# Where scale and shift of the second layer normalisation are applied: on rows by GpSimd, or on transposed columns by ScalarE

## The reference

```python
x = x + tanh(g_xattn) * attention(layernorm(x), ctx, ctx, ...)   # first normalisation: no scale, no shift
x = x + tanh(g_ffn) * experts(layernorm(x), ...)                 # inside experts, once more:
#   mu, var over the 256 features of a token
#   xn = (xf - mu) / sqrt(var + 1e-5) * ln_gamma + ln_beta       # second normalisation, scale and shift per feature
#   logits = xn @ Wr.T ; softmax ; top 2 of 8 experts per token
#   buf[expert, slot] = xn[token]        (640 slots for each expert)
#   h = silu(buf @ Wg) * (buf @ Wu) ; y = h @ W3.T
#   out[token] += weight * y             (two experts for each token)
```

## Time and profile before

| | us |
|---|---|
| median of 3 runs | 553.26 (552.57 to 554.41) |
| span of the profiled execution, first to last instruction | 547.9 |
| median less span: what lies around the instructions | 5.4 |

### The profile page before, as it was taken

How to read it: one execution, slowest core, us unless ns; L and a number is a source line. 1 busy time by engine, 2 the same in 40 slices (tenths; PEclk the granted TensorE clock), 3 DMA queues, 4 the chain that set the end, 5 groups by cost and what they waited for, 6 DMA issues and landing times. The chain is left out here.

```text
span 547.9 us, 10716 instructions
## 1 busy us (share of the span) xinstructions
PE 474.1 (87%) x3469; PEld 436.0 (80%) x3469; DVE 378.4 (69%) x942; ACT 299.3 (55%) x756; POOL 210.1 (38%) x271
## 2 busy tenths in 40 slices
PE   5599998899989776219979999999999999999990
PEld 4388887677767664219979999998999989999990
DVE  6878989999998998736758584484853757644340
ACT  3689778687778763316546463373732736424130
POOL 8536768687868556420120303202132021221121
PEclk9899999999999998559999999999999999999996
DMA  8858331314132511164626463255551554111011
GB/s 272 203 129 211 67 75 46 77 41 78 49 70 67 195 51 52 38 215 144 214 40 211 97 214 93 25 140 162 142 166 19 136 173 136 18 18 16 11 19 19
DMA packets 41137, 56.80 MB, mean 104 GB/s; under 512 B 3721, under 2 KB 38064, under 8 KB 39040
## 3 DMA queue, kind: packets, MB, share of 16 engines
q1 hardware_dynamic: 34656, 48.10, 30.2%
q0 software_dynamic: 6144, 8.07, 8.7%
q10 hardware_dynamic: 288, 0.00, 0.0%
HBM read 36.24 MB, written 16.19 MB: 96 GB/s over the span
## 5 line engine op out<-in xcount | busy, mean ns | idle before, releaser
L544 POOL DMA_INDIRECT out_tokens<-ysc,rows x32 | 50.6, 1581 | 252.8 <-DVE ysc L1142 181.0
L1431 PE MATMUL bank<-bXh,wh 128*128 128x384 f32 (+1 forms) x384 | 123.1, 321 | 7.8 <-PEq L1506 3.0
L1432 PE MATMUL bank<-bXl,wh 128*128 128x384 f32 (+1 forms) x384 | 122.3, 319 | 0.0
L1433 PE MATMUL bank<-bXh,wl 128*128 128x384 f32 (+1 forms) x384 | 122.3, 318 | 0.0
L752 ACT ACTIVATE sil<-bank 128x384 f32<-128x384 f32 (+1 forms) x96 | 43.8, 456 | 112.8 <-PE bank L1433 112.8
L1128 DVE TENSOR_TENSOR hF<-sil,bank 128x384 f32<-128x384 f32 (+1 forms) x96 | 48.9, 510 | 79.7 <-ACT sil L752 79.7
L635 ACT ACTIVATE p<-bank,nb 128x128 f32<-128x128 f32 x256 | 73.5, 382 | 32.0 <-DVE nb L927 31.9
L1431 PEld LDWEIGHTS bank<-bXh,wh 128*128 128x128 f32 x384 | 73.2, 190 | 9.1 <-issue 6.3
L1431 PE MATMUL bank<-wh,hH 128*128 128x256 f32 x256 | 73.1, 286 | 0.3 <-DVE ysc L1142 0.3
L1432 PEld LDWEIGHTS bank<-bXl,wh 128*128 128x128 f32 x384 | 73.1, 190 | 0.0
L1433 PEld LDWEIGHTS bank<-bXh,wl 128*128 128x128 f32 x384 | 73.0, 190 | 0.0
(11 more groups left out here) (146 smaller groups left out, 867.4 us busy)
## 6 DMA issues: line engine op xcount, KB each, us to landing
stage<-in_w12T SPq DMA_DIRECT2D x16, 1024.0 KB, 4.8
stage<-in_w3T SPq DMA_DIRECT2D x8, 1024.0 KB, 5.7
expert_rows<-padrow SPq DMA_DIRECT2D x8, 662.5 KB, 8.0
rows<-expert_rows SPq DMA_DIRECT2D x7, 662.5 KB, 4.3
kM<-k SPq DMA_DIRECT2D x64, 64.0 KB, 2.4
cT<-in_ctxT SPq DMA_DIRECT2D x8, 256.0 KB, 3.4
out_tokens<-x_all SPq DMA_DIRECT2D x8, 256.0 KB, 2.3
x_all<-in_x SPq DMA_DIRECT2D x2, 640.0 KB, 8.3
```

The source lines that it names most:

```text
L544: pool.indirect_dma_start(out=out, out_offset=bass.IndirectOffsetOnAxis(rows[par][:, c, D + E:ROW].bitcast(U32), 0), in_=ysc[par][:, c, :] ...
L1431: nc.tensor.matmul(out_ap, ah, bh, start=start, stop=False)
L1432: nc.tensor.matmul(out_ap, ah, bl, start=False, stop=False)
L1433: return nc.tensor.matmul(out_ap, al, bh, start=False, stop=stop)
```

## The change

The rows that are scattered and transposed hold only the plain normalised value, made by one operation with two per-row scalars. Scale and shift are applied where features lie on partitions: as `scale` and `bias` of ScalarE's copy out of the bank. They come from a small tile `aff` (128x4) in place of the two 128x256 tiles. In the experts ScalarE makes two copies of each transposed tile: the value in fp32 (`bXf`) and the high part, and VectorE subtracts from the first and no longer from the bank. The negative means are prepared by one more small GpSimd operation. The first normalisation is also one operation for each sequence (two for each block) on GpSimd. The loops over the middle blocks are unrolled; each of them ran once (TensorE, VectorE, GpSimd) or twice (ScalarE, SyncE).

The blocks of the diff are, in this order: SyncE's loads; GpSimd's `rstd1`, `normalize_inputs`, `norm2`, `normalize2`; ScalarE's `x2_columns` and `rows_high`; VectorE's `normalize2` of the last block and `rows_low`; TensorE's `rows_columns`.

```diff
-            for dst, src in ((bob, bo), (gab, gamma), (beb, beta)):
-                sp.dma_start(dst[:, :], src.partition_broadcast(P)).then_inc(ld_c, 16)
+            sp.dma_start(bob[:, :], bo.partition_broadcast(P)).then_inc(ld_c, 16)
+            sp.dma_start(aff[:, :, :], affine).then_inc(ld_c, 16)
...
             def rstd1(a, b):
                 pool.wait_ge(dve_mv1, b)
+                pool.tensor_scalar(nmu_all[:, a:b], mv_all[:, a:b, 0], -1.0, None, ALU.mult).then_inc(pool_ln1, 1)
...
             def normalize_inputs(n):
                 pool.wait_ge(pe_xT, n)
-                pool.tensor_tensor(xn1[:, :, :], x_all[:, bass.ds(n * SB * D, SB * D)].rearrange("p (i d) -> p i d", d=D),
-                                   mv_all[:, seqs, 0].unsqueeze(2).to_broadcast([P, SB, D]), ALU.subtract).then_inc(pool_xc, 1)
-                pool.wait_ge(pool_xc, n - 1)
-                pool.tensor_tensor(xn1[:, :, :], xn1[:, :, :], rs_all[:, seqs].unsqueeze(2).to_broadcast([P, SB, D]), ALU.mult)\
-                    .then_inc(pool_xn1, 1)
+                for j in range(SB):
+                    i = SB * n + j
+                    pool.tensor_scalar(xn1[:, j, :], x_tile(i), nmu_all[:, i:i + 1], rs_all[:, i:i + 1], ALU.add, ALU.mult)\
+                        .then_inc(pool_xn1, 1)
...
             def norm2(m, j):
                 pool.tensor_scalar(lnv[:, j:j + 1], mv2[:, j, 1:2], 1.0 + EPS, EPS * EPS, ALU.mult, ALU.add).then_inc(pool_rs2, 1)
-                pool.wait_ge(pool_rs2, 2 * i + 1)
+                pool.tensor_scalar(nmu2[:, j:j + 1], mv2[:, j, 0:1], -1.0, None, ALU.mult).then_inc(pool_rs2, 1)
+                pool.wait_ge(pool_rs2, 3 * i + 2)
...
             def normalize2(m, mpar, j, reuse):
-                r = xr[mpar][:, j, 0:D]
-                pool.tensor_tensor(r, x_tile(i), mv2[:, j, 0:1].to_broadcast([P, D]), ALU.subtract).then_inc(pool_xg, 1)
-                pool.wait_ge(pool_rs2, 2 * i + 2)
-                pool.wait_ge(pool_xg, 3 * i + 1)
-                pool.tensor_tensor(r, r, lnr[:, j:j + 1].to_broadcast([P, D]), ALU.mult).then_inc(pool_xg, 1)
-                pool.wait_ge(pool_xg, 3 * i + 2)
-                pool.tensor_tensor(r, r, gab[:, :], ALU.mult).then_inc(pool_xg, 1)
-                pool.wait_ge(pool_xg, 3 * i + 3)
-                pool.tensor_tensor(r, r, beb[:, :], ALU.add).then_inc(pool_xr, 1)
+                pool.wait_ge(pool_rs2, 3 * i + 3)
+                pool.tensor_scalar(xr[mpar][:, j, 0:D], x_tile(i), nmu2[:, j:j + 1], lnr[:, j:j + 1], ALU.add, ALU.mult).then_inc(pool_xr, 1)
...
             def x2_columns(m, bank):
-                act.activation(xnT[:, :, :], bank[:, :].rearrange("p (c t) -> p c t", c=DC), ACT.Copy).then_inc(act_x2T, 1)
+                for c in range(DC):
+                    ins = act.activation(xnT[:, c, :], bank[:, c * SB * T:(c + 1) * SB * T], ACT.Identity,
+                                         bias=aff[:, 1, c:c + 1], scale=aff[:, 0, c:c + 1])
+                ins.then_inc(act_x2T, 1)
...
             def rows_high(e, par, a):
-                act.activation(bXh[par][:, d, o:o + w], Xc[a % 2][:, 0:w], ACT.Copy).then_inc(act_bh, 1)
+                if not (isinstance(e, int) and e == 0 and a < 2):
+                    act.wait_ge(dve_bl, 4 * e + a - 1)
+                act.activation(bXf[a % 2][:, 0:w], Xc[a % 2][:, 0:w], ACT.Identity, bias=aff[:, 1, d:d + 1], scale=aff[:, 0, d:d + 1])
+                act.activation(bXh[par][:, d, o:o + w], Xc[a % 2][:, 0:w], ACT.Identity, bias=aff[:, 1, d:d + 1], scale=aff[:, 0, d:d + 1])\
+                    .then_inc(act_bh, 1)
...
             def normalize2(j):
-                dve.scalar_tensor_tensor(r, x_tile(i), mv2[:, j, 0:1], gab[:, :], ALU.subtract, ALU.mult).then_inc(dve_xg, 1)
-                dve.wait_ge(dve_xg, j + 1)
-                dve.scalar_tensor_tensor(r, r, lnr[:, j:j + 1], beb[:, :], ALU.mult, ALU.add).then_inc(dve_xr, 1)
+                dve.tensor_scalar(xr[mpar][:, j, 0:D], x_tile(i), mv2[:, j, 0:1], lnr[:, j:j + 1], ALU.subtract, ALU.mult).then_inc(dve_xr, 1)
...
             def rows_low(e, par, a):
-                dve.tensor_tensor(bXl[par][:, d, o:o + w], Xc[a % 2][:, 0:w], bXh[par][:, d, o:o + w].bitcast(F32), ALU.subtract)\
+                dve.tensor_tensor(bXl[par][:, d, o:o + w], bXf[a % 2][:, 0:w], bXh[par][:, d, o:o + w].bitcast(F32), ALU.subtract)\
...
             def rows_columns(e, par, use, a):
-                    pe.wait_ge(dve_bl, 4 * e + a - 1)
+                    pe.wait_ge(act_bh, 4 * e + a - 1)
```

More of the change, by code:

```diff
@@ L56, with gated_block @@
 LATE = 1.0e6
-def gated_block(nc, x, ctxT, gates, biases, wqT, wkT, wvT, woT, bo, gamma, beta, wrT, w12T, w3T, out):
+def gated_block(nc, x, ctxT, gates, biases, wqT, wkT, wvT, woT, bo, affine, wrT, w12T, w3T, out):
     with ExitStack() as top:
@@ L174, in gated_block @@
         hL = [sb(pc, f"hL{c}", [P, FT, w], F32R) for c, (_, w) in enumerate(CHUNKS)]
+        bXf = [sb(pc, f"bXf{i}", [P, 384], F32) for i in range(2)]
         sil = [sb(pc, f"sil{i}", [P, 384], F32) for i in range(2)]
@@ L294, in turn @@
                 load_ctx(n, par)
-                if isinstance(n, int) and n == 2:
+                if n == 2:
                     pad(range(E // 2, E))
@@ L301, in _ @@
             turn(2, 0)
[L302 to L305, removed]
+            for n in range(3, NSB):
+                turn(n, n % 2)
             load_stage(0, w12T[0, 0:P, :])
@@ L527, in _ @@
             body(3, 1, True, True, True, True, True, 1)
-            with pool.Fori(2, NSB // 2 - 1) as i:
-                body(2 * i, 0, True, True, True, True, True, i - 1)
-                body(2 * i + 1, 1, True, True, True, True, True, i)
+            for n in range(4, NSB - 2):
+                body(n, n % 2, True, True, True, True, True, n // 2 - 1 + n % 2)
             body(NSB - 2, 0, True, True, True, True, False, NSB // 2 - 2)
@@ L685, in _ @@
             body(1, 1, True, False, True, True)
-            with act.Fori(1, NSB // 2 - 1) as i:
-                body(2 * i, 0, True, True, True, True)
-                body(2 * i + 1, 1, True, True, True, True)
-            body(NSB - 2, 0, True, True, True, True)
+            act.wait_ge(ld_c, 16 * 2)
+            for n in range(2, NSB - 1):
+                body(n, n % 2, True, True, True, True)
             body(NSB - 1, 1, True, True, True, False)
@@ L1020, in _ @@
             stats1(0, SB)
-            dve.wait_ge(pool_ln1, 1)
+            dve.wait_ge(pool_ln1, 2)
             normalize_inputs(0)
@@ L1039, in _ @@
             body(1, 1, True, True, True, True, True)
-            with dve.Fori(2, NSB // 2 - 1) as i:
-                body(i, 0, True, True, True, True, True)
-                body(i, 1, True, True, True, True, True)
+            for n in range(4, NSB - 2):
+                body(n // 2, n % 2, True, True, True, True, True)
             body(NSB // 2 - 1, 0, True, True, True, True, True)
@@ L1377, in _ @@
             body(3, 1, True, True, True, True, True, 3)
-            with pe.Fori(2, NSB // 2 - 1) as i:
-                body(2 * i, 0, True, True, True, True, True, i + 1)
-                body(2 * i + 1, 1, True, True, True, True, True, i + 2)
-            body(NSB - 2, 0, True, True, True, True, True, NSB // 2)
+            for n in range(4, NSB - 1):
+                body(n, n % 2, True, True, True, True, True, (n + 1) // 2 + 1)
             body(NSB - 1, 1, True, True, True, True, False, None)
@@ L1531 @@
         "woT": a["L0_xattn_wo"].T, "bo": a["L0_xattn_bo"],
-        "gamma": a["L0_ffn_ln_gamma"], "beta": a["L0_ffn_ln_beta"],
+        "affine": _np.stack([a[f"L0_ffn_ln_{n}"].reshape(DC, P).T for n in ("gamma", "beta")], axis=1),
         "wrT": a["L0_ffn_Wr"].T,
```

23 lines of the change are left out of this document (12 added, 11 removed).

## The result

The changed kernel takes 559.57 us (559.21 to 560.56) against 552.98 for the kernel before on the same chip: a ratio of 1.0125, 95% interval 1.0098 to 1.0151. The forecast was 553.7 with 549 to 558.5 as its range. It missed by 5.9 us, on the slow side.

A forecast was written before the change was run, and what follows sets the result against it. TensorE was taken to bound the experts, TensorE and VectorE handing over work the attention. Span 547.9 - 4.8 attention + 4.95 experts - 0.3 tail + 0.3 start = 548.0, plus 5.4 around it 553.4, called 553.7; range 549 to 558.5 us.

The forecast's parts named there:

- Experts: +4.95: Experts part: 3.75 us at three borders plus 1.2 us at the first expert's start; range 3.55 to 6.
- 1.25 each: Borders behind experts 1, 3 and 5: four ScalarE operations take 1.91 us for 0.66, all on TensorE's path.
- The first border: Behind expert 0: TensorE waits for its own branch, longer than for VectorE, so no cost was added.
- TensorE's first multiplication of the next expert starts as that ends: Expert borders: VectorE's subtraction holds TensorE (304.73 and 304.72), so added copy time is on the path.
- Attention, -4.8: Attention bodies: 5.0 us less stall, less 0.2 for `values_rest`; first normalisation zero; range -9 to +2.
- the 5.0 of the sum: Attention, bodies 3 to 7: `nb` of step 3 stalls 1.0 us less in each of five bodies.
- TensorE's wait goes with the stall: Attention: a microsecond given back to VectorE is one given back to TensorE, up to 15.4 us.
- my slow rival: Attention, bodies 3 to 5: four gapless GpSimd operations block VectorE, 4.2 us back, 557.6; chance 0.32 shared with experts' upper end.
- GpSimd's operation, 1.0 us: Normalisation on GpSimd: one 128x256 operation with two per-row scalars takes 1.0 us; upper bound 1.6.
- more freed than 6.6 us: Attention rival: stalls fall 8 or 9 us, GpSimd's operation being short or VectorE getting in between; 549.5; chance 0.33 shared.
- The 5.4 around the span: Whole kernel: 5.4 us of time lie around the profiled span, added to 548.0 to give 553.4.
- The range: Whole kernel: 549 to 558.5 us, leaving out one in ten at each end.

The follow-up runs named there:

- b1_two_ops: Kernel before with only the experts' two ScalarE operations per tile (scale 1, shift 0): ratio 1.0176 to the kernel before, 9.7 us slower.
- a1_plain_experts: Changed kernel with one plain copy per tile in the experts again, scale and shift left out there: ratio 0.9912 to the kernel before.
- the second profile of before: Kernel before, unchanged, profiled once more: span 552.1 us, time 553.75 us.
- d1_gap_only: Kernel before with three more VectorE operations ahead of its branch, not waited for, nothing added on ScalarE: ratio 0.9997 to the kernel before.
- d2_gap_waited: Kernel before with three more VectorE operations that VectorE waits for ahead of its branch: ratio 1.0176 to the kernel before, 9.7 us slower.
- f1_else_first: Changed kernel with VectorE's branch and its signal `dve_h` ahead of the low parts of tiles 2 and 3: ratio 0.9921 to before, 548.68 us.
- u1_unrolled: Kernel before with the attention part's loops written out, nothing else: ratio 1.0020 to the kernel before, 1.1 us slower.
- a2_norm1_two_ops: `a1_plain_experts` with the first normalisation as before, two GpSimd operations on 128x512 per body: ratio 0.9969 to the kernel before.
- c1_fill: Changed kernel with ten added matmuls ahead of the wait at the borders of experts 2, 4 and 6: ratio 1.0137 to the kernel before.
- h2_fill_e1: `f1_else_first` with ten added matmuls ahead of TensorE's branch behind expert 0: ratio 0.9935 to the kernel before.
- h1_fill_both: `f1_else_first` with added matmuls at expert 0's start (52 and 8) and ahead of the branch at expert 1 (10): ratio 0.9875, 546.44 us.
- m1_rolled_fill: `f1_else_first` with the attention's loops as loops again and the 52, 8 and 10 added matmuls: ratio 0.9860 to before, 546.17 us.

## Why the prediction was wrong

**The step that failed: "Experts: +4.95".** The gaps in it were right: 1.27, 1.24 and 1.21 us at the three borders for a forecast of 1.25 each, and 1.23 at the start for 1.2. The price of one operation was too (0.56 and 0.67 us). What was missing, put at nothing without a reason, is the clock: two of the three gaps that grew to over 2 us are followed by a stretch at the lower clock, 3.2 to 3.5 us of it behind those of experts 2 and 6, 1.6 us lost in each. The two parts measured singly put the experts at 9.7 us (`b1_two_ops`) and, from `a1_plain_experts` to the changed kernel, 11.8. Against the second profile of before the rows give 9.9 (8.7 and the 1.2 of the start): 3.7 gaps, 1.2 the start, 3.3 the clock at 2 and 6, 0.6 a longer low stretch at expert 0 (4.5 for 3.2 us), 0.9 at the first border, and 0.2 not assigned. `d1_gap_only` and `d2_gap_waited` show that the idle time is the cause of the lower clock at 2 and 6; what remains between 9.9 and 11.8 is not settled, and the intervals (8.4 to 11.1 for the one run, some 9.7 to 13.9 for the other) overlap.

**The first border.** I wrote that TensorE's own branch is what it waits for behind expert 0, and longer than VectorE. That holds: VectorE's last operation ended at 276.07 and TensorE started at 277.63, and in `f1_else_first`, where VectorE's signal no longer waits for that operation, the gap is 3.52 us all the same. But the gap grew, by 0.45 against the second profile. It is 2.9 to 3.3 us in the eight profiles of kernels that make one copy of each tile, and 3.5 to 3.8 in the seven that make two and have no matmuls added ahead of this border. Why TensorE's own branch ends later with the second operation is open. `ysc` costs a further 0.41 there, since VectorE comes to it later; I had not looked at it.

**"TensorE's first multiplication of the next expert starts as that ends", that is VectorE's subtraction.** The size was right, the cause was not (`d1_gap_only`), and two of the three borders of the trace of before did not show it. Read rightly it would have shown the repair: the next chunk needs none of what VectorE waits for.

**Attention, -4.8.** The sum came true, 4.9 us (`a1_plain_experts`, which has the tail, the start and the written-out loops in it), by other terms, which is luck. From `u1_unrolled` to `a2_norm1_two_ops` the second normalisation and the tail give 2.8, not 5.1; the first gives 3.2, not zero; writing out the loops costs 1.1, not zero. Over the whole change the stalls of `nb` in step 3 fell by 6.8 us in five bodies, more than the 5.0 of the sum, but others came, and what I took from it, that TensorE's wait goes with the stall, failed: `u1_unrolled` has 4.2 us less of this stall and is no faster. The run without a gap, my slow rival, did no harm that shows: the kernel with it (`a1_plain_experts`) is 3.2 us faster than the one without (`a2_norm1_two_ops`), and no VectorE operation of step 5 in the five bodies stands for 3 us.

**GpSimd's operation, 1.0 us.** It takes 0.60. The Trainium skill's page GPSIMD Engine Reference, section Engine selection, by which I had estimated 0.2 us and dispatch, is not borne out as it stands: 0.60 us lies between its estimate and the 0.94 of the row. The rival that hung on it, more freed than 6.6 us, did not come: its condition held in part, its consequence did not. With what the Trainium skill's page SBUF — State Buffer, section Who interferes with whom, says, that the blocked engine waits for the other's whole instruction, the stalls shown above agree (VectorE goes on when the one operation is done: 123.34 and 123.31); the longer ones of the earlier trace rows remain beyond it.

**The 5.4 around the span.** It is 1.7. This did no harm to the forecast, since the sum was set on the median, but it hid that the profiled execution was a short one, and with it the lower clock at expert 1.

**The range.** Its upper end was taken from stalls in the attention. No term in it was the clock, although had a start of expert 0 whose matmul took 0.66 us for 0.45 in the earlier trace rows, behind idle time.

## What to carry to other kernels

Price a new gap in front of a busy TensorE with what follows it too: here a gap that grew from 1 to over 2 us cost 1.2 us by itself and 1.6 us of lower clock behind it at two of three borders. Before adding work behind a wait, ask what the waiting engine really needs: a signal that stood behind operations it does not depend on made these gaps, and moving it took more away (11 us) than the change had cost (6.9). And where a change has a gain and a loss in different stages, run each stage alone: the 4.9 us of this one were hidden behind its loss.

## What the runs showed that I had not expected

- VectorE's branch ran ahead of the operations before it: TensorE was released 1.0 us before VectorE's last operation ended (`d1_gap_only`), and only waits hold it.
- The idle time that TensorE's own branch ends is 2.9 to 4.1 us at one border or two of each kernel; at the others what is left of it is short. It is at expert 1 in most kernels, at 1 and 4 in `c1_fill` (3.98 us) and `h2_fill_e1` (4.13; at 1 there 2.26, behind the added matmuls), at 2 in `h1_fill_both` (3.58) and `m1_rolled_fill` (3.72). Each time matmuls were added to the code it moved or a second one came. Loading of instructions would fit: in the traces a DMA packet of 16 KB of the kind `instruction` (queue q8) starts within each of the 19 such gaps of 2.9 us and more, as at 274.24 in the kernel before (gap from 274.12 to 277.15). But such a packet also starts where VectorE ends a shorter gap (374.92, expert 4), and no run took one away, so the cause is not shown.
- A gap of 2.5 to 2.6 us at expert 4 was not followed by the lower clock in any of four profiles, gaps of 2.25 to 2.6 at experts 2 and 6 in all of them. What tells them apart is open.
